# A four-layer block on one core: the layer norm of the next batch is taken later in the MLP stage

## The chip, the cores and the metric

One core of a Trainium2 chip runs one program. The time is that of the device in microseconds (us), the median of three runs. TensorE is called PE (its weight loads PEld), VectorE DVE, ScalarE ACT, GpSimd POOL, SyncE SP. The program is one long chain of stages, parted by barriers, so that what a stage takes longer the program takes longer.

## The reference

Four layers follow each other on x of 8 batches x 256 tokens x 512 features: an attention to a context, an attention over channels, a transformer layer (self attention, cross attention, MLP), and a recurrent block. The change is in the MLP of the third:

```python
ln_out = layernorm(x, ln3_s, ln3_b)
mlp_out = gelu(ln_out @ w1 + b1) @ w2 + b2      # w1: 512 x 2048, w2: 2048 x 512
return x + mlp_out
```

## The kernel before

`token_mlp` is the stage. It goes over the 8 batches (256 rows each) one after the other, and in each over 8 chunks of 256 hidden features. Every engine has its own instruction queue, written out by hand in the order of `for b, n in order(...)`: b is the batch, n the chunk. Products are made in three passes of rounded high and low parts (`_hi`, `_lo`), and so each operand has to be split on DVE or POOL ahead of the product.

In chunk n PE makes `hidden(b, n)` (24 matmuls, L2212), then, in two chunks of each batch, a `turn` (4 transposes, L2199) of the normalised rows of the next batch, then `outputs` of the chunk three back (12 matmuls, L2227), as `Y_LAG` is 3; so outputs(b, 4) is the last of batch b ahead of hidden(b+1, 0), and outputs(b, 5) to (b, 7) stand in the first chunks of b+1. `hidden(b, 0)` first waits for `ln_split` of its batch.

For a chunk of hidden, ACT evicts the sums (`evict`, L2267 and L2270) as the values `pre` and their squares; DVE makes 0.044715 times the square plus 1 (called squared1 here, L2374); POOL multiplies by `pre` (cube, L2183); ACT takes the tanh (`bend`, L2276); DVE multiplies (`gelu`, L2366); ACT rounds (`round_hidden`, L2281); POOL takes the rest (`split_hidden`, L2158). In chunk n each engine does squared1, cube and evict of n, and bend, gelu, rounding and rest of n-1.

The layer norm of the next batch b+1 is made beside batch b: SP loads its rows (L2122); DVE takes `statistics` (L2315) and `moment` (L2322), POOL the power -0.5 (`power`, L2166), DVE `normalise` (L2329) into xn; PE turns xn in two halves; ACT keeps each half with the scale and bias applied (`keep_turned`, L2253); DVE splits it (`split_turned`: a cast at L2336, a subtraction at L2338, which raises `ln_split`). `TURN_STEPS` names the two chunks in which the turns stand; the splits stand one chunk behind them. `add_bias` on POOL (L2170) adds the last bias to the rows, and in batch 0 it waits for all weights to be split, since it writes where they were staged; the load of batch b+2 waits for it.

Batch 0 has more to do. Of the weights the first two quarters of w1 are there when the stage begins. The rest comes in twelve halves of 512 KB through three staging buffers, in this order:

```python
HALVES = [(n, i, k) for n, i in (("w2", 0), ("w1", 2), ("w2", 1), ("w1", 3), ("w2", 2), ("w2", 3)) for k in range(2)]
```

SP loads them (L2132; the load of batch 1's rows stands behind half 4), ACT rounds two of them in each of chunks 0 to 5 (L2259), and DVE splits two in the same chunk (L2348), behind its gelu and ahead of its layer norm work. The load of half k, from 3 on, waits for the split of half k-3. PE waits for the halves that it needs: hidden 4 for halves 2 and 3, hidden 6 for 6 and 7, outputs 0, 2, 4 and 6 for 0 and 1, 4 and 5, 8 and 9, 10 and 11.

Of the kernel before, what the change touches and what calls it, by code (L numbers as in the profile page):

```python
# [12 lines left out]
BATCH, TOK, FEAT = 8, 256, 512  # L13
# [33 lines left out]
def make_identity(pool, ident, sem):  # L47

    pool.memset(ident[:, :], 0.0).then_inc(sem, 1)
    pool.wait_ge(sem, 1)  # L50
    pool.affine_select(out=ident[:, :], in_=ident[:, :], compare_op=ALU.not_equal, fill=1.0, base=0,
                       pattern=[[-1, P]], channel_multiplier=1).then_inc(sem, 1)
# [1975 lines left out]
def token_mlp(nc, semaphores, x, w1_d, w2_d, ln_cols, b1, b2, out, ahead, here, following):  # L2028
# [4 lines left out]
    Y_LAG = 3  # L2033

    HALVES = [(n, i, k) for n, i in (("w2", 0), ("w1", 2), ("w2", 1), ("w1", 3), ("w2", 2), ("w2", 3)) for k in range(2)]
    TURN_STEPS = (2, 4)
    with ExitStack() as ctx:
        def sb(name, shape, dtype=F32):
            return ctx.enter_context(nc.sbuf_tensor("mlp_" + name, shape, dtype))
# [46 lines left out]
        def of(b, per_batch, k, unit=1):  # L2086

            return at(b + 2, per_batch, k, unit)

        def piece_of(i, part):  # L2090
            return (w1_hi, w1_lo)[part][:, :, i * FEAT:(i + 1) * FEAT]
# [7 lines left out]
        def order(drain):  # L2099

            for g in range(BATCH * CHUNKS + drain):
                yield g // CHUNKS, g % CHUNKS

        def before(b, n, steps):
            g = b * CHUNKS + n - steps
            return g // CHUNKS, g % CHUNKS
# [42 lines left out]
        @block.gpsimd  # L2149
        def _(pool):  # L2150
            make_identity(pool, ident, ident_made)
            pool.memset(half_power[:, :], -0.5).then_inc(const_made, 1)
            pool.memset(eps[:, :], 1e-5).then_inc(const_made, 1)
            pool.wait_ge(const_made, 2)

            def split_hidden(b, k):
                pool.wait_ge(hid_rounded, of(b, CHUNKS, k))
                pool.tensor_tensor(hid_lo[k % RING][:, :, :], pre[k % RING], hid_hi[k % RING][:, :, :].bitcast(F32),  # L2158
                                   ALU.subtract).then_inc(hid_split, 1)

            def power(b):
                pool.wait_ge(counted, of(b, 2, 1))
                pool.wait_ge(normalised, of(b - 1, 1, 0))
                pool.tensor_tensor(var_eps[:, :], moments[:, :, 1], eps[:, :], ALU.add).then_inc(powered, 1)
                pool.wait_ge(powered, of(b, 2, 0))
                pool.tensor_tensor(rstd[:, :], var_eps[:, :], half_power[:, :], ALU.pow).then_inc(powered, 1)  # L2166

            def add_bias(b):
                pool.wait_ge(added, of(b - 1, 1, 0))
                pool.tensor_tensor(xb, xs[b % 2][:, :, :], b2_row[:, :].unsqueeze(1).to_broadcast([P, TT, FEAT]),  # L2170
                                   ALU.add).then_inc(biased, 1)

            power(0)
            pool.wait_ge(cols_loaded, 48)
            for b, n in order(1):
                if b == 0 and n == 6:
                    pool.wait_ge(half_split, len(HALVES))
                    add_bias(b)
                elif 0 < b < BATCH and n == Y_LAG + 1:
                    add_bias(b)  # L2180
                if b < BATCH:
                    pool.wait_ge(squared1, of(b, CHUNKS, n))
                    pool.tensor_tensor(cube[n % RING], cube[n % RING], pre[n % RING], ALU.mult).then_inc(cubed, 1)  # L2183
                if b or n:
                    split_hidden(*before(b, n, 1))
                if n == 0 and b + 1 < BATCH:
                    power(b + 1)

        @block.tensor
        def _(pe):  # L2190
# [45 lines left out]
            for b, n in order(Y_LAG):  # L2236
                if b < BATCH:
                    if n == 0:
                        pe.wait_ge(ln_split, of(b, 2, 1))
                    hidden(b, n)  # L2240
                if n in TURN_STEPS and b + 1 < BATCH:
                    turn(b + 1, TURN_STEPS.index(n))
                if b or n >= Y_LAG:
# [3 lines left out]
        def _(act):  # L2247
# [45 lines left out]
            for b, n in order(1):  # L2293
# [7 lines left out]
                if b or n:  # L2301
                    round_hidden(*before(b, n, 1))
                if n in TURN_STEPS and b + 1 < BATCH:
                    keep_turned(b + 1, TURN_STEPS.index(n))
                if 0 < b < BATCH and n == Y_LAG:
# [4 lines left out]
        @block.vector  # L2310
        def _(dve):
            def statistics(b):
                dve.wait_ge(loaded[b % 2], 16 * (b // 2 + 1))
                for m in range(TT):
                    ins = dve.bn_stats(stats[:, m, :], xs[b % 2][:, m, :])  # L2315
                ins.then_inc(counted, 1)

            def moment(b):
                dve.wait_ge(counted, of(b, 2, 0))
                dve.wait_ge(normalised, of(b - 1, 1, 0))  # L2320
                for m in range(TT):
                    ins = dve.bn_aggr(moments[:, m, :], stats[:, m, :])  # L2322
                ins.then_inc(counted, 1)

            def normalise(b):
                dve.wait_ge(powered, of(b, 2, 1))
                dve.wait_ge(turned, of(b - 1, 2, 1))
                for m in range(TT):
                    ins = dve.tensor_scalar(xn[:, m, :], xs[b % 2][:, m, :], moments[:, m, 0:1], rstd[:, m:m + 1],  # L2329
                                            ALU.subtract, ALU.mult)  # L2330
                ins.then_inc(normalised, 1)

            def split_turned(b, i):
                here = slice(2 * i, 2 * i + 2)
                dve.wait_ge(turned_kept, of(b, 2, i))
                dve.tensor_copy(ln_hi[b % 2][:, here, :], ln_raw[:, here, :]).then_inc(ln_rounded, 1)  # L2336
                dve.wait_ge(ln_rounded, of(b, 2, i))
                dve.tensor_tensor(ln_lo[b % 2][:, here, :], ln_raw[:, here, :], ln_hi[b % 2][:, here, :].bitcast(F32),  # L2338
                                  ALU.subtract).then_inc(ln_split, 1)

            def split_piece(i):
                dve.wait_ge(piece_hi, i + 1)
                dve.tensor_tensor(piece_of(i, 1), ahead.pieces[i][:, :, :], piece_of(i, 0).bitcast(F32),
                                  ALU.subtract).then_inc(piece_split, 1)

            def split_half(k):
                dve.wait_ge(half_hi, k + 1)
                dve.tensor_tensor(half_of(k, 1), stages[k % 3], half_of(k, 0).bitcast(F32), ALU.subtract).then_inc(half_split, 1)  # L2348

            statistics(0)  # L2350
            moment(0)
            normalise(0)
            split_piece(0)
            split_turned(0, 0)
            split_turned(0, 1)
            split_piece(1)
            def add_rows(b):
                dve.wait_ge(y_used, of(b, CHUNKS, CHUNKS - 1))
                dve.wait_ge(biased, of(b, 1, 0))
                dve.wait_ge(stored, of(b - 1, 1, 0, 16))  # L2360
                dve.scalar_tensor_tensor(out=res, in0=ps_y[:, :, :], scalar=0.5, in1=xb,
                                         op0=ALU.mult, op1=ALU.add).then_inc(added, 1)

            def gelu(b, k):
                dve.wait_ge(bent, of(b, CHUNKS, k))
                dve.scalar_tensor_tensor(out=pre[k % RING], in0=cube[k % RING], scalar=1.0,  # L2366
                                         in1=pre[k % RING], op0=ALU.add, op1=ALU.mult).then_inc(gelled, 1)

            for b, n in order(1):
                if 0 < b < BATCH and n == Y_LAG:  # L2370
                    add_rows(b - 1)
                if b < BATCH:
                    dve.wait_ge(squared, of(b, CHUNKS, n))
                    dve.tensor_scalar(cube[n % RING], cube[n % RING], 0.044715, 1.0, ALU.mult, ALU.add).then_inc(squared1, 1)  # L2374
                if b or n:
                    gelu(*before(b, n, 1))
                if b == 0 and n < len(HALVES) // 2:
                    split_half(2 * n)
                    split_half(2 * n + 1)
                if b + 1 < BATCH:  # L2380
                    if n == 0:
                        statistics(b + 1)
                        moment(b + 1)
                    elif n == 1:
                        normalise(b + 1)
                    elif n - 1 in TURN_STEPS:
                        split_turned(b + 1, TURN_STEPS.index(n - 1))
            add_rows(BATCH - 1)
# [1104 lines left out]
```

## Time and profile before

| | |
|---|---|
| median of three runs | 3719.94 us (3717.66 to 3721.94) |
| the profiled execution | 3721.94 us, its span 3719.9 us |
| PE busy | 3444.8 us (93% of the span) |
| DVE busy | 2339.9 us (63%) |
| POOL busy | 2012.5 us (54%) |
| ACT busy | 1835.1 us (49%) |
| mean granted clock of PE | 0.969 |
| the MLP stage | PE's first matmul at 2348.46 us, the last store issued at 2744.77 us |

Times in the rows are microseconds from the start of the span. Matmuls overlap, so the time from one start to the next says how long one takes, and the printed duration is longer. The granted clock is a share of 2.4 GHz; there are two levels, 0.5 and 1. In a row of a timeline the bracket tells how long the engine sat idle ahead of the instruction, and for what. DVE's printed durations overlap the next start by some 0.08 us.

### The profile page before, as it was taken

The page shows a single profiled execution, that of the slowest core. Times are in us where ns is not written, and L with a number is a line of the kernel's source. Part 1 is how long each engine was busy: PE and PEld are TensorE (multiplying, and loading weights), DVE is VectorE, ACT ScalarE, POOL GpSimd, SP SyncE. Part 2 cuts the span into 40 slices and gives each one's busy share as a digit, 9 for nine tenths or more (in the row PEclk, how much of TensorE's full clock was granted, in tenths as well). Part 3 has the DMA queues.
Part 4 walks back from the last instruction along what each step waited for, and adds up shares of the span by engine and source line. Part 5 has one row for each costly group of instructions (what it writes and reads, how often), then busy time and mean ns, then how long its engine had stood idle before and what let it go on. Part 6 is the DMA issues. An engine that isn't in the chain of part 4 may idle for free. (4 is left out here: it accounts for less than half of the span.)

```text
span 3719.9 us, 59815 instructions
## 1 busy us (share of the span) xinstructions
PE 3444.8 (93%) x23544; PEld 2669.8 (72%) x23544; DVE 2339.9 (63%) x2892; ACT 1835.1 (49%) x4242; POOL 2012.5 (54%) x1088
## 2 busy tenths in 40 slices
PE   8989999999999999979989998799987888889978
PEld 6878778877877887558877776699975655656544
DVE  2455665565566556657778787555535677787776
ACT  2134664565456446556766776455532333333322
POOL 2235665575567556425556666355534566666653
PEclk9999999999999999989999999799998899999989
DMA  4231211121122111120021111200040000000000
GB/s 139 98 128 46 81 57 59 58 70 58 48 70 69 59 46 58 39 98 33 30 75 52 41 41 55 88 23 24 18 147 6 13 18 1 18 18 18 13 18 12
DMA packets 114302, 189.91 MB, mean 51 GB/s; under 512 B 17904, under 2 KB 36848, under 8 KB 113392
## 3 DMA queue, kind: packets, MB, share of 16 engines
q1 hardware_dynamic: 111856, 182.00, 14.4%
q8 instruction: 183, 3.00, 0.3%
q10 hardware_dynamic: 2176, 4.19, 0.3%
q14 instruction: 87, 0.71, 0.1%
HBM read 161.01 MB, written 25.17 MB: 50 GB/s over the span
## 5 line engine op out<-in xcount | busy, mean ns | idle before, releaser
L1025 POOL TENSOR_TENSOR l_pr<-l_pr,l_inv 128x1024 f32<-128x1024 f32 x256 | 479.8, 1895 | 383.6 <-DVE l_inv L1087 383.6
L895 ACT ACTIVATE l_pr<-l_ps_s,l_top 128x512 f32<-128x512 f32 x512 | 348.6, 690 | 353.0 <-DVE l_top L1083 271.9
L1529 POOL TENSOR_TENSOR tok_pr<-tok_pr,tok_ma 128x1024 f32<-128x1024 f32 x128 | 304.4, 2400 | 280.2 <-DVE tok_pr L1907 280.2
L2790 POOL TENSOR_TENSOR rec_rs<-rec_sE,rec_rT 128x1024 f32<-128x1024 f32 x128 | 326.7, 2555 | 215.8 <-DVE rec_sE L3278 166.8
L1020 POOL TENSOR_TENSOR l_x_lo<-ahead_piece,l_x_hi 128x1024 fp32r<-128x1024 f32 (+1 forms) x97 | 294.0, 3031 | 154.2 <-ACT l_x_hi L879 154.2
L1083 DVE TENSOR_REDUCE l_top<-l_ps_s 128x2 f32<-128x1024 f32 x256 | 304.1, 1218 | 10.5 <-PE l_ps_s L669 10.5
L3278 DVE TENSOR_TENSOR_SCAN rec_sE<-rec_wE,rec_ps_v 128x1024 f32<-128x1024 f32 x128 | 292.7, 2287 | 5.5 <-POOL rec_rs L2790 1.1
L679 PE MATMUL l_ps_t<-l_ident,l_pr 128*128 128x128 f32 x2048 | 275.3, 277 | 10.8 <-POOL l_pr L1025 4.8
L679 PEld LDWEIGHTS l_ps_t<-l_ident,l_pr 128*128 128x128 f32 x2048 | 225.6, 141 | 78.1 <-issue 60.7
L1779 ACT ACTIVATE tok_pr<-tok_pr,tok_shift 128x256 f32<-128x256 f32 x512 | 253.7, 498 | 15.8 <-DVE tok_shift L1915 14.5
L630 PE MATMUL l_ps_b<-l_x_hi,l_w_lo 128*128 128x256 f32 x784 | 226.7, 289 | 0.0
L630 PE MATMUL l_ps_b<-l_x_hi,l_w_hi 128*128 128x256 f32 x784 | 221.2, 282 | 0.0
L630 PE MATMUL l_ps_b<-l_x_lo,l_w_hi 128*128 128x256 f32 x784 | 221.0, 282 | 0.0
L3275 DVE TENSOR_TENSOR rec_ps_v<-rec_ps_v,rec_kT 128x1024 f32<-128x1024 f32 x128 | 156.7, 1225 | 72.5 <-ACT rec_kT L3143 71.5
L1915 DVE TENSOR_REDUCE tok_shift<-tok_pr 128x4 f32<-128x1024 f32 x128 | 155.5, 1216 | 47.6 <-POOL tok_pr L1529 45.5
L1091 DVE COPY l_pT<-l_ps_t 128x512 f32<-128x512 f32 x256 | 174.3, 681 | 2.9 <-PE l_ps_t L679 2.6
L900 ACT ACTIVATE l_pT<-l_ps_t 128x512 f32<-128x512 f32 x256 | 152.5, 596 | 22.7 <-PE l_ps_t L679 22.6
L1615 PE MATMUL tok_ps_t<-tok_ident,tok_pr 128*128 128x128 f32 x1024 | 138.7, 279 | 24.7 <-DVE tok_pT L1920 17.5
L1907 DVE TENSOR_TENSOR tok_pr<-tok_ps_s,tok_mk 128x1024 f32<-128x1024 f32 x128 | 155.7, 1217 | 5.3 <-PE tok_ps_s L1604 5.3
L1615 PEld LDWEIGHTS tok_ps_t<-tok_ident,tok_pr 128*128 128x128 f32 x1024 | 113.6, 142 | 54.9 <-issue 35.8
L657 PE MATMUL l_ps_b<-l_wv_lo,l_x_hi 128*128 128x256 f32 x512 | 149.4, 292 | 3.5 <-DVE l_wv_lo L1074 2.1
L630 PEld LDWEIGHTS l_ps_b<-l_x_hi,l_w_lo 128*128 128x128 f32 x784 | 148.2, 189 | 2.7 <-issue 1.0
(507 smaller groups left out, 9752.3 us busy)
## 6 DMA issues: line engine op xcount, KB each, us to landing
ahead_piece<-x SPq DMA_DIRECT2D x63, 512.0 KB, 3.9
ahead_piece<-in_c SPq DMA_DIRECT2D x63, 512.0 KB, 4.7
ahead_rows<-x SPq DMA_DIRECT2D x22, 512.0 KB, 3.8
ahead_piece<-in_L_w_qk SPq DMA_DIRECT2D x16, 512.0 KB, 6.0
x<-tok_xb SPq DMA_DIRECT2D x16, 512.0 KB, 2.8
l_xt<-in_xT SPq DMA_DIRECT2D x8, 512.0 KB, 6.5
l_ct<-in_cT SPq DMA_DIRECT2D x8, 512.0 KB, 7.6
l_xn<-in_x SPq DMA_DIRECT2D x8, 512.0 KB, 4.8
```

The lines of the kernel that those rows point to most:

```text
L630: mm = pe.matmul(bank[:, here], w[:, part, half * SLOTS + s, :], x[b % 2][:, s, here], start=(s == 0 and w is w_lo), stop=(s == SLOTS - 1 ...
L679: mm = pe.transpose(ps_t[h][:, m, :], pr[t][:, h, m * P:(m + 1) * P], ident[:, :])
L895: act.activation(pr[t][:, h, :], ps_s[:, t % 2, h, :], ACT.Exp, bias=top[:, t, h:h + 1], accum_out=mass[:, t, h:h + 1]).then_inc(exped, 1)
L1020: pool.tensor_tensor(x_lo[b % 2][:, which, :], rows, x_hi[b % 2][:, which, :].bitcast(F32), ALU.subtract).then_inc(x_split, 2 if source is ...
L1025: pool.tensor_tensor(pr[t][:, :, :], pr[t][:, :, :], inv[:, t, :].unsqueeze(2).to_broadcast([P, 2, FEAT]), ALU.mult).then_inc(scaled, 1)
L1083: dve.tensor_reduce(top[:, t, :], ps_s[:, t % 2, :, :], AXIS.X, ALU.max, negate=True).then_inc(topped, 1)
L1091: dve.tensor_copy(pT[1][:, :, t * P:(t + 1) * P], ps_t[1][:, :, :]).then_inc(turned_kept[1], 1)
L1529: pool.tensor_tensor(tile, tile, ma[u][:, :, :].rearrange("p t k -> p (t k)").unsqueeze(1).to_broadcast([P, 2, TT * TOK]), ALU.add).then_i ...
L1615: mm = pe.transpose(ps_t[:, i, t, m * P:(m + 1) * P], pr[n % RING][:, i, m, t * P:(t + 1) * P], ident[:, :])
L1779: ins = act.activation(tile, tile, ACT.Exp, bias=shift[n % RING][:, i, m:m + 1], accum_out=mass[n // 2 % 2][:, m, n % 2 * 2 + i:n % 2 * 2 ...
L2790: pool.tensor_tensor(rs[j % 2][:, :, :], sE[j % 2][:, :, :], rT[s][:, :, :], ALU.mult).then_inc(rs_made, 1)
L3278: dve.tensor_tensor_scan(sE[j % 2][:, :, :].rearrange("p c t -> p (c t)"), wE[s][:, :, :].rearrange("p c t -> p (c t)"), ps_v[j % 2][:, :, ...
```

## The change

The layer norm work of the next batch is put later within a batch: statistics and moment, and the power on POOL, from chunk 0 to chunk 1; normalise from chunk 1 to 2; the two turns (with keep_turned) from chunks 2 and 4 to 4 and 6; and so the two split_turned from chunks 3 and 5 to 5 and 7. In batch 0, add_bias on POOL goes from chunk 6 to chunk 7. No instruction is added or taken away.

```diff
@@ -2033,7 +2033,7 @@
     Y_LAG = 3
 
     HALVES = [(n, i, k) for n, i in (("w2", 0), ("w1", 2), ("w2", 1), ("w1", 3), ("w2", 2), ("w2", 3)) for k in range(2)]
-    TURN_STEPS = (2, 4)
+    TURN_STEPS = (4, 6)
     with ExitStack() as ctx:
         def sb(name, shape, dtype=F32):
             return ctx.enter_context(nc.sbuf_tensor("mlp_" + name, shape, dtype))
@@ -2173,7 +2173,7 @@
             power(0)
             pool.wait_ge(cols_loaded, 48)
             for b, n in order(1):
-                if b == 0 and n == 6:
+                if b == 0 and n == 7:
                     pool.wait_ge(half_split, len(HALVES))
                     add_bias(b)
                 elif 0 < b < BATCH and n == Y_LAG + 1:
@@ -2183,7 +2183,7 @@
                     pool.tensor_tensor(cube[n % RING], cube[n % RING], pre[n % RING], ALU.mult).then_inc(cubed, 1)
                 if b or n:
                     split_hidden(*before(b, n, 1))
-                if n == 0 and b + 1 < BATCH:
+                if n == 1 and b + 1 < BATCH:
                     power(b + 1)
 
         @block.tensor
@@ -2378,10 +2378,10 @@
                     split_half(2 * n)
                     split_half(2 * n + 1)
                 if b + 1 < BATCH:
-                    if n == 0:
+                    if n == 1:
                         statistics(b + 1)
                         moment(b + 1)
-                    elif n == 1:
+                    elif n == 2:
                         normalise(b + 1)
                     elif n - 1 in TURN_STEPS:
                         split_turned(b + 1, TURN_STEPS.index(n - 1))
```

## Rows read from the trace of the kernel before

**Rows 1.** Busy time by stretch: us, PE, PEld, DVE, ACT, POOL, clock, DMA share, GB/s

```profile
2366.00:2388.00 22.00, 6.70 (x37) 6.52 (x37) 14.20 (x16) 9.18 (x16) 9.09 (x6) 0.61 0.46 140
...
2520.00:2560.00 40.00, 40.00 (x260) 36.15 (x259) 20.33 (x23) 20.78 (x46) 20.90 (x16) 1.00 0.07 27
```

**Rows 2.** Waits in the stage: total us, times, longest

```profile
ACT ahead_piece L2267 <- PE mlp_ps_h L2212: 58.2, 60, 3.6
...
PE mlp_ps_t L2199 <- DVE mlp_xn L2329: 15.3, 1, 15.3
```

**Rows 3.** Timeline of PE, batch 0: start, us, instruction, idle before

```profile
2366.76 0.28 PE L2212 MATMUL mlp_ps_h<-mlp_ln_hi,mlp_w_hi 128*128 128x256 f32 x1
2382.34 1.08 PE L2199 MATMUL mlp_ps_t<-mlp_ident,mlp_xn 128*128 128x128 f32 x4 [15.30 <-DVE mlp_xn L2329]
2383.07 0.56 PE L2212 MATMUL mlp_ps_h<-mlp_ln_hi,mlp_w_lo 128*128 128x256 f32 x1
...
2413.82 0.28 PE L2212 MATMUL mlp_ps_h<-mlp_ln_hi,mlp_w_lo 128*128 128x256 f32 x1
```

**Rows 4.** Timeline of DVE, batch 0

```profile
2374.51 1.29 DVE L2315 BATCH_NORM_STATS2 mlp_stats<-mlp_xs 128x6 f32<-128x512 f32 x2 [7.34 <-DMA mlp_xs<-x]
...
2380.26 1.94 DVE L2329 TENSOR_SCALAR mlp_xn<-mlp_xs,mlp_moments,mlp_rstd 128x512 f32<-128x512 f32 x2
2382.12 0.41 DVE L2374 TENSOR_SCALAR ahead_piece<-ahead_piece 128x512 f32<-128x512 f32 x1
...
2383.06 2.29 DVE L2348 TENSOR_TENSOR mlp_w_lo<-mlp_xb_res,mlp_w_hi 128x1024 fp32r<-128x1024 f32 x1
2385.27 2.30 DVE L2348 TENSOR_TENSOR mlp_w_lo<-mlp_spare,mlp_w_hi 128x1024 fp32r<-128x1024 f32 x1
2389.88 0.43 DVE L2374 TENSOR_SCALAR ahead_piece<-ahead_piece 128x512 f32<-128x512 f32 x1 [2.31 <-ACT ahead_piece L2270]
...
2407.86 2.79 DVE L2338 TENSOR_TENSOR mlp_ln_lo<-mlp_ln_raw,mlp_ln_hi 128x512 fp32r<-128x512 f32 x1
```

**Rows 5.** Timeline of the queue of SP, batch 0

```profile
2367.62 0.46 SPq L2122 DMA_DIRECT2D mlp_xs<-x  x1
```

**Rows 6.** Timeline of PE, steady batch: hidden, outputs, hidden begin

```profile
2488.73 0.28 PE L2212 MATMUL mlp_ps_h<-mlp_ln_hi,mlp_w_lo 128*128 128x256 f32 x1
...
2491.55 0.40 PE L2227 MATMUL mlp_ps_y<-mlp_w_lo,mlp_hid_hi 128*128 128x512 f32 x1
...
2494.36 0.28 PE L2212 MATMUL mlp_ps_h<-mlp_ln_hi,mlp_w_lo 128*128 128x256 f32 x1
```

**Rows 7.** Timeline of ACT and DVE in the same steady batch

```profile
2491.76 0.84 ACT L2267 ACTIVATE ahead_piece<-mlp_ps_h,mlp_b 128x256 f32<-128x256 f32 x2 [0.72 <-PE mlp_ps_h L2212]
...
2493.36 0.43 DVE L2374 TENSOR_SCALAR ahead_piece<-ahead_piece 128x512 f32<-128x512 f32 x1 [3.89 <-ACT ahead_piece L2270]
2493.88 1.82 DVE L2366 SCALAR_TENSOR_TENSOR ahead_piece<-ahead_piece 128x512 f32<-128x512 f32 x1
2495.63 0.41 DVE L2336 CAST mlp_ln_hi<-mlp_ln_raw 128x512 fp32r<-128x512 f32 x1
2496.07 0.69 DVE L2338 TENSOR_TENSOR mlp_ln_lo<-mlp_ln_raw,mlp_ln_hi 128x512 fp32r<-128x512 f32 x1
```

**Rows 8.** Timeline of POOL, batch 0: add_bias

```profile
2407.49 2.61 POOL L2170 TENSOR_TENSOR mlp_xb_res<-ahead_rows,mlp_b 128x1024 f32<-128x1024 f32 x1
```

**Rows 9.** Timelines of DVE and PE where PE waited for a split

```profile
2357.55 0.69 DVE L2338 TENSOR_TENSOR mlp_ln_lo<-mlp_ln_raw,mlp_ln_hi 128x512 fp32r<-128x512 f32 x1
...
2358.29 0.39 PE L2212 MATMUL mlp_ps_h<-mlp_ln_hi,mlp_w_lo 128*128 128x256 f32 x1
```

**Rows 10.** Context stage: a wait of PE, and stretches as in rows 1

```profile
78.87 0.50 PE L163 MATMUL l_ps_d<-l_cv_hi,l_prT_lo 128*128 128x512 f32 x1 [2.56 <-DVE l_prT_lo L375]
...
78.90:83.90 5.00, 5.00 (x18) 4.14 (x19) 2.53 (x3) 0.00 (x0) 5.00 (x3) 0.66 0.62 190
118.70:123.70 5.00, 5.00 (x31) 4.49 (x32) 3.23 (x3) 0.00 (x0) 5.00 (x3) 1.00 0.58 188
```

## Prediction

> **What bounds the kernel now.** I read the page first for the shares (PE 93% of the span), then the busy time by stretch for the one stage that the diff touches, then who waited for whom in it, and last the timeline of single instructions. In the body of the stage PE is busy in 40.00 of 40.00 us at the full clock, DVE in 20.33 and POOL in 20.90 [rows 1]. So a microsecond of stall on PE is a microsecond of the program, and work on DVE or POOL is free as long as nothing on PE waits for it. Of the waits, ACT's for PE's sums (58.2 us in 60 waits) is the mark of a stage that PE paces; the only long wait of PE itself is one of 15.3 us for xn [rows 2].
>
> That wait belongs to batch 0. PE has run chunks 0 to 2 of hidden by 2366.8, reaches turn(1, 0), and starts it only at 2382.34. The next chunk of hidden begins at 2383.07, and hidden(1, 0), the first work of batch 1, at 2413.82 [rows 3]. DVE shows why: statistics(1) waits 7.34 us for the rows of batch 1, which SP issued at 2367.62 behind two halves of weights [rows 4, 5], starts at 2374.51, and normalise(1) follows at 2380.26, behind the next chunk and two splits of weights [rows 4].
>
> **What the change does at the start.** Everything is one chunk later for statistics and normalise, and two later for the turns. The rows of batch 1 still land when they did, since SP's order is the same: DVE is held at statistics(1) until about 2374.5 again. But in front of that wait it has now done chunk 1's squared1 and gelu and the splits of halves 2 and 3, which before came after it. Behind it come chunk 2, halves 4 and 5, and normalise(1): the same list with each number one higher. So normalise(1) ends, and turn(1, 0) starts, near 2382.3 as before. The difference is what PE has done by then: hidden 3, outputs 0 and hidden 4 lie ahead of the turn, 3 x 2.81 us (outputs takes 2494.36 - 2491.55 = 2.81 us, hidden 2491.55 - 2488.73 = 2.82, [rows 6]). Before, the first of these, hidden 3, even ran for the most part at the lower clock of 1.2 GHz (the mean granted over 2366 to 2388 is 0.61 of 2.4 GHz, [rows 1]), behind PE's long wait.
>
> Does PE keep this? From 2382.34 it has left: two turns (about 0.4 each), four outputs and three hiddens, 7 x 2.81 + 0.8 = 20.5 us, so it could be at hidden(1, 0) at 2402.8. But it waits there for ln_split, that is for split_turned(1, 1) on DVE. DVE's list between 2382.1 and that split was, before, four chunks, eight halves and both split_turned, ending 2407.86 + 2.79 = 2410.65 [rows 4]. Now it is five chunks, six halves and the same two splits. Two halves less is 2 x 2.21 = 4.4 us (2383.06 to 2385.27), DVE's wait of 2.31 at 2389.88 (for the sums that PE made at half clock) is gone, and a chunk more is 0.94 (2382.12 to 2383.06, when its inputs are ready, [rows 4]) to 2.27 (2493.36 to 2495.63, when POOL's cube runs beside it, [rows 7]): 2404.9 to 2406.2. And chunk 7's squared1 now stands between the turn and the split: behind gelu 5 ACT rounds, keeps the turned half and evicts, and DVE waits for all three. Before, that wait was 3.89 us behind chunk 4, of which ACT itself waited 0.72 for PE; 3.2 us remain, since PE is ahead now [rows 7]. That gives 2408.1 to 2409.4; I take 2408.8, and so **5.0 us** gained at hidden(1, 0) against 2413.82. The bounds: 8.5 at best (2402.8 plus the 2.5 us of the next part), nothing at worst.
>
> add_bias(0) moves on POOL from chunk 6 to chunk 7. Before, it ran at 2407.49 for 2.61 us, and the split beside it took 2.79 instead of 0.69 us [rows 4, 7, 8]. It will again run just ahead of that split, so I leave its 2.1 us in. The Trainium skill (SBUF — State Buffer, Who interferes with whom) has GpSimd and certain VectorE instructions take one port pair in turn for a whole instruction; the trace agrees, as the split ends only after add_bias does. By that rule a collision costs up to the full 2.61 us, and the gain would be 5.0 with it and some 7.1 without.
>
> **What the change does at every batch's end.** This is the part I hold to be decisive. hidden(b+1, 0) comes after outputs(b, 4), and waits for both halves of ln. Before, the second split_turned was done at chunk 5, with two chunks in hand. Now it stands in chunk 7, the last, behind that chunk's squared1 and gelu. The trace has exactly this pattern one step early: at chunk 5 of a batch, a step behind a turn. PE ends its hidden at 2491.55, does outputs, and wants the next hidden at 2494.36 [rows 6]. ACT evicts at 2491.76, squared1 runs at 2493.36, gelu at 2493.88 (1.82 us), the cast at 2495.63 and the second half of the split at 2496.07 [rows 7]. From the start of that instruction to PE's start is 0.74 us, where PE did wait for it (2357.55 to 2358.29, [rows 9]): 2496.81. So PE stalls 2496.81 - 2494.36 = **2.45 us**. Nothing else is in PE's queue that it could do: outputs(b, 5) stands behind hidden(b+1, 0). Behind the stalled hidden wait ACT's next evict, and through it DVE and POOL, so all shift together and the pattern repeats. There are seven boundaries; the first is in the sum above, six remain: 6 x 2.45 = 14.7 us. Bounds of one: 1.1 if squared1 and gelu take 0.94 instead of 2.27 (above), and 4.5 if the split takes 2.79 as beside add_bias [rows 4].
>
> **The clock.** PE's stall in this dense work can lower its clock. The context stage has four waits of 2.56 us in dense matmuls; behind the one that ended at 78.87 the granted clock over 5 us was 0.66, so two thirds of the 5 us ran at 1.2 instead of 2.4 GHz, while behind the one at 118.7 it was 1.00 [rows 10]. One such fall is 0.34 x 5 = 1.7 us of full-speed work lost. I take two falls in six, 3.4 us; bounds 0 and 6 x 1.7 = 10.2.
>
> **What costs nothing.** In batches 1 to 6 statistics and moment (1.29 us and a trifle) move into chunk 1 and normalise (at most 1.94, [rows 4]) into chunk 2; DVE is idle half of the time there, PE needs xn only at chunk 4, and POOL's power moves with them. Without that cover each would still have two chunks, 11 us, before the turn. The turn instructions on PE are the same number. The load of batch 2 waits for add_bias(0), which now comes at about 2407 and not 2407.49, and its first reader stands a chunk later. No DMA is added.
>
> **Sum.** -5.0 + 14.7 + 3.4 = +13.1 us. The profiled execution took 3721.94; 3735.0 by it. The median of the three runs is 3719.94, 2.0 lower, so 3733.
>
> **Rivals.**
> - The clock falls at nearly every boundary: -5.0 + 14.7 + 10.2 = +19.9, 3740. For it: the fall behind 78.87. Against: the 1.00 behind an equal wait. 0.14.
> - Batch 0 gives nothing back, since weights or DVE hold it as long as before: 14.7 + 3.4 = +18.1, 3738. For it: halves are chained through DVE, ACT and loads. Against: PE is two sets further by 2382, and two halves are already split. This is also the case in which the change does not remove the wait but moves it. 0.10.
> - Batch 0 gives all of 8.5 and no fall of the clock: +6.2, 3726. 0.10.
> - The other side: the stall at the boundary does not come, because the last split is done before PE wants it. Then only batch 0 counts, -5.0 to -11.0 (8.5 and the first boundary's 2.45), 3709 to 3715. It decides only if the chain from evict to split, 5.0 us, fits in outputs' 2.8; even with the shorter pair it takes 3.7. With the whole 8.5 gained, a stall under 0.2 us would be needed to be faster by 0.2%. 0.07.
> - My forecast, around +13: 0.59.
>
> **Numbers.** 0.2% of this kernel is 7.4 us, about what can be told from no change: slower means over 3727.4, faster under 3712.5. From the cases: slower 0.75 (forecast, clock, nothing back, less some where batch 0 gives more), same 0.17, faster 0.08. The range runs from 3722 (batch 0's best, smaller stalls) to 3742 (clock at most boundaries); the last case and the extremes, about 2 in 10, are left out.
>
> **What would show it.** In the profile after: the 15.3 us wait of PE for xn shrinks to one of about 3 us at turn(1, 0), near the same time 2382; PE waits about 2.5 us, seven times, in front of L2212 for L2338 on DVE, once per batch at a pitch of 48.3 us (8 x 5.63 for the sets, 0.8 for two turns, and the stall); hidden(1, 0) starts near 2409; the clock over some of the 5 us behind the stalls is under 1.00. The prediction is wrong if those waits are missing or under 1 us, if hidden(1, 0) starts well before 2405, or if DVE's rows of batch 1 land later than 2374.5 because half 5 is now issued beside them.

## The result, and the profile after

The changed kernel takes 3744.06 us (median of four runs, 3743.09 to 3751.37), against 3720.94 before on the same chip: 1.0066 times as long, interval 1.0048 to 1.0084, so slower by 0.66% and clear of the noise. The forecast had the direction; the time lies 2 us over its range of 3722 to 3742. The profiled execution took 3744.32 us, 22.4 more than that of before.

The page of the changed kernel, its span and the busy time of the engines:

```profile
span 3742.3 us, 59815 instructions
...
PE 3457.7 (92%) x23544; PEld 2678.3 (72%) x23544; DVE 2332.8 (62%) x2892; ACT 1833.5 (49%) x4242; POOL 2011.9 (54%) x1088
```

PE is busy 13 us longer with the same 23544 matmuls: more of them ran at the lower clock. The waits within the stage (total us, times, longest):

```profile
PE mlp_ps_h L2212 <- DVE mlp_ln_lo L2338: 20.6, 8, 6.8
...
PE mlp_ps_y L2227 <- POOL mlp_hid_lo L2158: 4.7, 2, 4.2
...
PE mlp_ps_y L2227 <- DVE mlp_xb_res L2361: 2.7, 6, 0.5
...
DVE mlp_stats L2315 <- DMA mlp_xs<-x: 2.0, 1, 2.0
...
PE mlp_ps_t L2199 <- DVE mlp_xn L2329: 0.4, 1, 0.4
```

The wait of 15.3 us for xn is 0.4 now [rows 2], and DVE waits 2.0 and not 7.3 us for the rows of batch 1 [rows 4]. In their place stand eight waits of PE for the last split (one of them is the wait of batch 0's start, 0.2 us), and six for L2361, add_rows, which nobody had forecast.

To leave out what differs between two runs ahead of the stage (the profile after reaches it 2.7 us sooner), I take the stage by itself: from PE's first matmul in it to the first of the next stage. Before, on PE's timeline:

```profile
2348.46 0.90 PE L59 MATMUL mlp_ps_h<-mlp_ident 128*128 128x128 f32 x3 [5.39 <-POOL mlp_ident L51]
...
2749.27 1.11 PE L59 MATMUL rec_ps_acc<-rec_ident 128*128 128x128 f32 x4 [5.79 <-POOL rec_ident L51]
```

After, with the starts of outputs 0, the first turn and hidden(1, 0):

```profile
2345.78 1.54 PE L59 MATMUL mlp_ps_h<-mlp_ident 128*128 128x128 f32 x6 [5.39 <-POOL mlp_ident L51]
...
2370.90 0.77 PE L2227 MATMUL mlp_ps_y<-mlp_w_lo,mlp_hid_hi 128*128 128x512 f32 x1 [4.25 <-POOL mlp_hid_lo L2158]
...
2379.46 0.63 PE L2199 MATMUL mlp_ps_t<-mlp_ident,mlp_xn 128*128 128x128 f32 x4 [0.38 <-DVE mlp_xn L2329]
...
2406.97 0.58 PE L2212 MATMUL mlp_ps_h<-mlp_ln_hi,mlp_w_lo 128*128 128x256 f32 x1 [6.75 <-DVE mlp_ln_lo L2338]
...
2771.17 1.12 PE L59 MATMUL rec_ps_acc<-rec_ident 128*128 128x128 f32 x4 [5.78 <-POOL rec_ident L51]
```

So the stage took 2749.27 - 2348.46 = 400.81 us and takes 2771.17 - 2345.78 = 425.39: 24.6 more. hidden(1, 0) starts 61.19 us behind the first matmul, and started at 2413.82 - 2348.46 = 65.36 [rows 3]: batch 0 gives 4.2 back, where 5.0 was forecast. DVE's timeline in batch 0 shows what hidden(1, 0) waits for:

```profile
2371.59 1.28 DVE L2315 BATCH_NORM_STATS2 mlp_stats<-mlp_xs 128x6 f32<-128x512 f32 x2 [1.96 <-DMA mlp_xs<-x]
...
2377.35 1.97 DVE L2329 TENSOR_SCALAR mlp_xn<-mlp_xs,mlp_moments,mlp_rstd 128x512 f32<-128x512 f32 x2
...
2397.59 0.69 DVE L2366 SCALAR_TENSOR_TENSOR ahead_piece<-ahead_piece 128x512 f32<-128x512 f32 x1
2401.34 1.90 DVE L2374 TENSOR_SCALAR ahead_piece<-ahead_piece 128x512 f32<-128x512 f32 x1 [3.07 <-ACT ahead_piece L2270]
2403.16 0.68 DVE L2366 SCALAR_TENSOR_TENSOR ahead_piece<-ahead_piece 128x512 f32<-128x512 f32 x1
2403.77 1.48 DVE L2336 CAST mlp_ln_hi<-mlp_ln_raw 128x512 fp32r<-128x512 f32 x1
2405.28 1.63 DVE L2338 TENSOR_TENSOR mlp_ln_lo<-mlp_ln_raw,mlp_ln_hi 128x512 fp32r<-128x512 f32 x1
```

Its rows come at 2371.59, normalise at 2377.35 and the turn at 2379.46, as the forecast had it (33.7 us into the stage, 33.9 before). At the end DVE waits 3.07 us between gelu 5 and squared1 of chunk 7, and from there squared1 (1.90 us, 0.42 in the chunk before), the cast (1.48) and the subtraction (1.63) are long, each beside an instruction of POOL. PE stands idle for 6.75 us.

A later boundary, as batch 4 ends and batch 5 begins, on PE: outputs(4, 4), hidden(5, 0), the next outputs, outputs(5, 0) and hidden(5, 4):

```profile
2604.39 0.40 PE L2227 MATMUL mlp_ps_y<-mlp_w_lo,mlp_hid_hi 128*128 128x512 f32 x1
...
2609.63 0.38 PE L2212 MATMUL mlp_ps_h<-mlp_ln_hi,mlp_w_lo 128*128 128x256 f32 x1 [2.28 <-DVE mlp_ln_lo L2338]
...
2612.57 0.40 PE L2227 MATMUL mlp_ps_y<-mlp_w_lo,mlp_hid_hi 128*128 128x512 f32 x1
...
2630.07 0.50 PE L2227 MATMUL mlp_ps_y<-mlp_w_lo,mlp_hid_hi 128*128 128x512 f32 x1 [0.45 <-DVE mlp_xb_res L2361]
...
2632.97 0.28 PE L2212 MATMUL mlp_ps_h<-mlp_ln_hi,mlp_w_lo 128*128 128x256 f32 x1
```

and on DVE: chunk 7 with the split, then chunk 2 with normalise and add_rows:

```profile
2606.19 0.43 DVE L2374 TENSOR_SCALAR ahead_piece<-ahead_piece 128x512 f32<-128x512 f32 x1 [3.73 <-ACT ahead_piece L2270]
2606.71 1.81 DVE L2366 SCALAR_TENSOR_TENSOR ahead_piece<-ahead_piece 128x512 f32<-128x512 f32 x1
2608.44 0.41 DVE L2336 CAST mlp_ln_hi<-mlp_ln_raw 128x512 fp32r<-128x512 f32 x1
2608.89 0.69 DVE L2338 TENSOR_TENSOR mlp_ln_lo<-mlp_ln_raw,mlp_ln_hi 128x512 fp32r<-128x512 f32 x1
...
2625.62 0.43 DVE L2374 TENSOR_SCALAR ahead_piece<-ahead_piece 128x512 f32<-128x512 f32 x1 [1.81 <-ACT ahead_piece L2270]
...
2627.89 0.99 DVE L2329 TENSOR_SCALAR mlp_xn<-ahead_rows,mlp_moments,mlp_rstd 128x512 f32<-128x512 f32 x2
2628.80 1.21 DVE L2361 SCALAR_TENSOR_TENSOR mlp_xb_res<-mlp_ps_y,mlp_xb_res 128x1024 f32<-128x1024 f32 x1
```

In the kernel before, at the same place of a batch, add_rows on DVE and outputs of chunk 3 on PE:

```profile
2523.77 1.21 DVE L2361 SCALAR_TENSOR_TENSOR mlp_xb_res<-mlp_ps_y,mlp_xb_res 128x1024 f32<-128x1024 f32 x1
...
2525.76 0.40 PE L2227 MATMUL mlp_ps_y<-mlp_w_lo,mlp_hid_hi 128*128 128x512 f32 x1
```

The reader is to see two things. From outputs to hidden PE takes 2609.63 - 2604.39 = 5.24 us, and took 2.81 [rows 6]: 2.43 of stall for the split that starts at 2608.89. And in chunk 3 outputs waits until add_rows, 1.21 us from 2628.80, has emptied the sums; add_rows stands behind normalise in DVE's queue; before, it ended 0.8 us ahead of outputs. The clock, by stretches of 5 us behind two of the stalls (columns as in rows 1):

```profile
2457.50:2462.50 5.00, 4.94 (x27) 4.85 (x28) 0.00 (x1) 0.28 (x1) 1.14 (x1) 0.66 0.00 0
...
2609.60:2614.60 5.00, 4.97 (x33) 4.60 (x34) 0.23 (x1) 1.83 (x5) 1.11 (x1) 1.00 0.00 0
```

Behind five of the six short stalls, and behind the long one, the granted clock is 0.66 to 0.68; behind the one at 2609.6 it is 1.00. hidden(5, 0) there takes 2612.57 - 2609.63 = 2.94 us; behind the others the same 24 matmuls take 4.16 to 4.46. Where they take 4.16, the outputs behind them are slow too: from one hidden(b, 0) to the next (called the pitch of a batch) it is 49.17 us behind 2609.63 and 50.67 to 50.70 behind the other four that a batch follows, so one fall of the clock costs 1.5 us.

### The profile page after: what moved, and what is told of

Its sections match the earlier page's. It is cut to its first block and busy times, and to the rows that moved or that the text cites. A ratio compares the mean times of both kernels' runs of the same rounds, so it can differ in the third digit from the quotient of the medians.

```text
span 3742.3 us, 59815 instructions
## 1 busy us (share of the span) xinstructions
PE 3457.7 (92%) x23544; PEld 2678.3 (72%) x23544; DVE 2332.8 (62%) x2892; ACT 1833.5 (49%) x4242; POOL 2011.9 (54%) x1088
## 3 DMA queue, kind: packets, MB, share of 16 engines
q10 hardware_dynamic: 2176, 4.19, 0.3%
## 5 line engine op out<-in xcount | busy, mean ns | idle before, releaser
L1083 DVE TENSOR_REDUCE l_top<-l_ps_s 128x2 f32<-128x1024 f32 x256 | 303.9, 1217 | 10.6 <-PE l_ps_s L669 10.5
L679 PE MATMUL l_ps_t<-l_ident,l_pr 128*128 128x128 f32 x2048 | 275.5, 277 | 10.7 <-POOL l_pr L1025 4.6
L1779 ACT ACTIVATE tok_pr<-tok_pr,tok_shift 128x256 f32<-128x256 f32 x512 | 253.7, 497 | 15.7 <-DVE tok_shift L1915 14.6
L2212 PE MATMUL mlp_ps_h<-mlp_ln_hi,mlp_w_lo 128*128 128x256 f32 x512 | 148.1, 289 | 20.6 <-DVE mlp_ln_lo L2338 20.6
L2183 POOL TENSOR_TENSOR ahead_piece<-ahead_piece 128x512 f32<-128x512 f32 x64 | 87.5, 1368 | 140.3 <-DVE ahead_piece L2374 140.3
L2374 DVE TENSOR_SCALAR ahead_piece<-ahead_piece 128x512 f32<-128x512 f32 x64 | 31.1, 486 | 198.4 <-ACT ahead_piece L2270 198.4
```

The source lines that it names most:

```text
L679: mm = pe.transpose(ps_t[h][:, m, :], pr[t][:, h, m * P:(m + 1) * P], ident[:, :])
L1083: dve.tensor_reduce(top[:, t, :], ps_s[:, t % 2, :, :], AXIS.X, ALU.max, negate=True).then_inc(topped, 1)
L1779: ins = act.activation(tile, tile, ACT.Exp, bias=shift[n % RING][:, i, m:m + 1], accum_out=mass[n // 2 % 2][:, m, n % 2 * 2 + i:n % 2 * 2 ...
```

## The experiments

The times are medians on the chip, beside runs of the kernel before on the same chip (3720.2 to 3721.2 in these), to which the ratios belong. Stages are from PE's first matmul of the stage to that of the next, each in one profile; "hidden(1, 0)" is its start from that first matmul. Four profiles with the same order in batch 0 (changed, first_batch_only, statistics_back, filled_stall) have it at 61.2 to 61.6. Many of the intervals of the ratios overlap, so small differences between two of the kernels are read from the rows of the stage and not from the whole time.

| kernel | time, us | ratio to before, interval | stage | hidden(1, 0) |
|---|---|---|---|---|
| before | 3719.94 | 1 | 400.8 | 65.4 |
| changed | 3744.06 | 1.0066 [1.0048, 1.0084] | 425.4 | 61.2 |
| first_batch_only | 3717.71 | 0.9991 [0.9982, 1.0] | 398.2 | 61.3 |
| later_batches_only | 3745.52 | 1.0076 [1.0062, 1.009] | 424.5 | - |
| statistics_back | 3740.29 | 1.0057 [1.0044, 1.0071] | 418.2 | 61.6 |
| turns_4_5 | 3715.72 | 0.9992 [0.9983, 1.0001] | 395.2 | 55.3 |
| filled_stall | 3740.51 | 1.0052 [1.0038, 1.0066] | 417.9 | 61.2 |
| split_ahead | 3719.97 | 0.9998 [0.9989, 1.0007] | 400.0 | 58.6 |
| first_batch_4_5 | 3711.20 | 0.9977 [0.9968, 0.9987] | 391.5 | 56.0 |
| rows_before_half_3 | 3712.29 | 0.998 [0.9971, 0.9989] | 393.2 | 57.8 |
| bias_at_6 | 3743.45 | 1.0061 [1.0049, 1.0073] | 426.9 | 62.5 |
| rows_early_turns_3_5 | 3709.14 | 0.997 [0.9959, 0.9981] | 389.8 | 54.4 |
| rows_early_turns_4_5 | 3711.91 | 0.9973 [0.9964, 0.9983] | 390.3 | 54.8 |

**first_batch_only** takes the change in batch 0 alone (statistics and power stand in the chunk STATISTICS(b), normalise in NORMALISE(b)):

```diff
-    TURN_STEPS = (4, 6)
+    TURN_STEPS = lambda b: (4, 6) if b == 0 else (2, 4)
+    STATISTICS = lambda b: 1 if b == 0 else 0
+    NORMALISE = lambda b: 2 if b == 0 else 1
```

> The change in batch 0 alone; batches 1 to 7 keep the order of before. Theory (three costs at each later boundary, a gain in batch 0): hidden(1, 0) starts 61.2 us behind PE's first matmul of the stage instead of 65.4, one fall of the clock of 1.5 us behind the long stall in front of it, nothing after: 2.7 us under before, 3718. Rival (batch 0 gives nothing back once the noise of its loads is taken out, and the gain of 4.2 us was read from one profile): within 1 us of before.

```profile
2347.27 1.12 PE L59 MATMUL mlp_ps_h<-mlp_ident 128*128 128x128 f32 x4 [5.39 <-POOL mlp_ident L51]
...
2408.55 0.58 PE L2214 MATMUL mlp_ps_h<-mlp_ln_hi,mlp_w_lo 128*128 128x256 f32 x1 [6.51 <-DVE mlp_ln_lo L2340]
...
2745.51 0.90 PE L59 MATMUL rec_ps_acc<-rec_ident 128*128 128x128 f32 x3 [5.79 <-POOL rec_ident L51]
```

398.2 us, 2.6 less than before; hidden(1, 0) starts at 61.3, and no wait follows it. In the stage the gain of batch 0 is there and small: 4.1 us sooner at hidden(1, 0), less 1.5 for the fall of the clock behind the long stall. By the whole time, 0.9991, the interval just reaches 1.0, so it is barely told from none.

**later_batches_only** is its complement (turns in 2 and 4 for b = 0, in 4 and 6 for the rest, and so on, add_bias(0) in chunk 6).

> Batch 0 as before, batches 1 to 6 changed. Theory: six stalls of PE of 2.43 us in front of hidden(b+1, 0) with 0.12 us of restart (15.3), six of 0.74 us in chunk 3 for add_rows (4.4), and a fall of the clock of 1.5 us behind five of the six (7.6): 27.3 us over before, 3748. Rival (the falls and the chunk 3 stalls hang on a phase that batch 0 of the changed kernel set): 15.3 us over before, 3736.

PE's waits from 2400 to 2725:

```profile
PE mlp_ps_h L2214 <- DVE mlp_ln_lo L2340: 13.7, 6, 2.3
PE mlp_ps_y L2229 <- DVE mlp_xb_res L2363: 2.7, 6, 0.5
```

Six stalls of 2.3 and six of 0.5 us are there with batch 0 as it was, so they don't hang on it. The stage came 23.7 us over before, not 27.3: the clock fell behind three of the six stalls, not five, and one fall is 1.5 us (a pitch of 50.7 against 49.2). The times of both parts, -2.6 and +23.7, make 21.1 of the 24.6; two falls less account for most of the rest.

**statistics_back** puts statistics and power in chunk 0 and normalise in chunk 1 again for b > 0, with the turns still in 4 and 6:

```diff
+    STATISTICS = lambda b: 1 if b == 0 else 0
+    NORMALISE = lambda b: 2 if b == 0 else 1
```

> The changed kernel, but in batches 1 to 6 statistics, power and normalise are back in chunks 0 and 1; the turns stay in 4 and 6. Theory: normalise ahead of add_rows makes the stall of 0.74 us in chunk 3, so the six go and the other costs stay: 4.4 us under the changed kernel, 3739.7, and no wait of PE for L2361. Rival (that stall comes from the phase behind the boundary stall, or from the missing turn in chunk 2, which gave add_rows 0.4 us more): the waits stay or shrink only in part, 3742 to 3744.

```profile
PE mlp_ps_h L2214 <- DVE mlp_ln_lo L2340: 20.1, 7, 6.4
```

That is all of PE's waits there: the six for add_rows are gone, and the pitch of a batch without a fall is 48.44 us (2653.26 to 2701.70) against 49.17 (2609.63 to 2658.80): 0.73 us each. Statistics and power went back together with normalise, but statistics in chunk 1 can't be what delays add_rows: behind it DVE waits 1.81 us for ACT at squared1 of chunk 2 (2625.62 above). So normalise's place makes that stall. The stage is 7.2 us shorter, of which 4.4 is this, and the rest in the main that the clock fell behind three of the six short stalls and not five.

**turns_4_5** has `TURN_STEPS = (4, 5)` in the changed kernel and nothing else.

> The changed kernel with the second turn in chunk 5 instead of 6, so that the last split_turned stands in chunk 6. Theory: all stalls in front of hidden(b+1, 0) go (6.75 + 6 x 2.55), and with them the falls of the clock (7 x 1.5); the six of 0.74 us stay: 3744.1 - 6.8 - 15.3 - 10.5 = 3711.5, 9 us faster than before. Rival (the falls of the clock come from the 0.46 us waits or from elsewhere, not from these stalls): 3722, and the clock still falls in most batches.

PE's two kinds of waits, at hidden(1, 0) and at outputs(1, 0):

```profile
2395.98 0.39 PE L2212 MATMUL mlp_ps_h<-mlp_ln_hi,mlp_w_lo 128*128 128x256 f32 x1 [1.34 <-DVE mlp_ln_lo L2338]
...
2416.41 0.50 PE L2227 MATMUL mlp_ps_y<-mlp_w_lo,mlp_hid_hi 128*128 128x512 f32 x1 [0.45 <-DVE mlp_xb_res L2361]
```

No wait stands at the six later boundaries, the clock is 1.00 from 2410 to 2730, and the stage is 395.2, 30.2 us less than changed (32.6 expected: hidden(1, 0) comes 5.9 sooner and not 6.8, as 1.3 us of wait stayed, and there were six falls to save, not seven). Six waits for add_rows stay, without any boundary stall ahead of them. The second turn's place, one chunk, carries more than the whole loss of 24.6; what is left of the change gains 5.6 us of stage on the kernel before. The whole time (0.9992, its interval reaches 1.0001) doesn't show that gain clearly, and the 9 us that were expected didn't come.

**split_ahead** leaves the turns in 4 and 6, but in chunk 7 DVE does the split first:

```diff
             for b, n in order(1):
+                if n == 7 and b + 1 < BATCH:
+                    split_turned(b + 1, 1)
...
-                    elif n - 1 in TURN_STEPS:
-                        split_turned(b + 1, TURN_STEPS.index(n - 1))
+                    elif n == 5:
+                        split_turned(b + 1, 0)
```

> The changed kernel with one instruction pair moved: in chunk 7 DVE does split_turned(b+1, 1) ahead of squared1 and gelu and not behind them; the turns stay in chunks 4 and 6. Theory (the stall is the place of the split behind squared1 and gelu, not the place of the turn): no stall at the six boundaries, about 1.5 us left at the first, no falls of the clock; the six of 0.74 us stay. Stage about 395 us as with the turns in chunks 4 and 5, 3715. Rival (a turn in chunk 6 is too late for ACT and PE as well): a stall of 1 us or more at each boundary, stage over 402.

DVE in a later batch (split, then squared1 of chunk 7), and the last split of batch 0:

```profile
2450.01 0.71 DVE L2336 CAST mlp_ln_hi<-mlp_ln_raw 128x512 fp32r<-128x512 f32 x1 [1.61 <-ACT mlp_ln_raw L2253]
2450.76 0.69 DVE L2338 TENSOR_TENSOR mlp_ln_lo<-mlp_ln_raw,mlp_ln_hi 128x512 fp32r<-128x512 f32 x1
2452.12 0.43 DVE L2376 TENSOR_SCALAR ahead_piece<-ahead_piece 128x512 f32<-128x512 f32 x1 [0.67 <-ACT ahead_piece L2270]
...
2402.10 2.72 DVE L2338 TENSOR_TENSOR mlp_ln_lo<-mlp_ln_raw,mlp_ln_hi 128x512 fp32r<-128x512 f32 x1
```

The split is done at 2451.4, squared1 starts at 2452.12 unhindered, and PE waits at no later boundary. A turn in chunk 6 is early enough; it was the queue that made the split late. At the first boundary the guess of 1.5 us was wrong: 3.3 stayed, since the split took 2.72 us beside add_bias, and the clock fell behind that stall (0.66 over 5 us). The stage is 400.0 and not 395, much as before the change.

**filled_stall** lets PE work in the stall:

```diff
                     if n == 0:
+                        if b:
+                            pe.wait_ge(turned_kept, of(b, 2, 1))
+                            keep_busy(pe, ps_t[0][:, 0, 0:P], ident, 18)
                         pe.wait_ge(ln_split, of(b, 2, 1))
```

> The changed kernel, and PE makes 18 transposes of the identity into a bank that nobody reads, in front of its wait for ln_split in batches 1 to 7, so that it works in most of the stall. Theory (the clock falls because PE is idle there): hidden(b+1, 0) starts at the same times as far as DVE sets them, the 1.5 us falls behind the six short stalls go, and the stage from PE's first matmul to that of the next stage takes some 9 us less than the 425.4 of the changed kernel: 3735. Rival (the falls have another cause, such as the waits of 0.46 us in chunk 3, which stay): no less than 423, 3742 to 3744.

The second hidden(b, 0) behind the transposes, and the stretch from 2410 to 2730, then the same stretch of the changed kernel:

```profile
2460.36 0.39 PE L2212 MATMUL mlp_ps_h<-mlp_ln_hi,mlp_w_lo 128*128 128x256 f32 x1 [0.33 <-DVE mlp_ln_lo L2341]
...
2410.00:2730.00 320.00, 315.31 (x2038) 283.86 (x2039) 145.29 (x171) 151.81 (x335) 156.40 (x121) 1.00 0.05 19
```

```profile
2410.00:2730.00 320.00, 303.57 (x1890) 272.29 (x1890) 142.70 (x169) 149.66 (x330) 153.89 (x119) 0.97 0.05 19
```

The mean clock of the stretch goes from 0.97 to 1.00, all later batches have a pitch of 49.18 us, and the stage is 7.5 us shorter, though each boundary still takes as long and PE has more to do. That is five falls of 1.5 us; the 9 us expected counted six. At hidden(1, 0) the 18 transposes left 4.19 us of wait, and behind it the clock still fell (0.67 over 5 us). The whole times alone (1.0052 and 1.0066, with intervals that overlap) wouldn't tell the two kernels apart. The cause of the falls behind the short stalls is PE's idleness in them. The Trainium skill (TensorE: Matmul & The Clock Gate, What's actually happening) says that the clock gate is set by how busy PE has been recently; the trace agrees, with a mean of 0.97 where PE idled at the six boundaries and 1.00 where they were filled. Over four kernels with these stalls (changed, later_batches_only, statistics_back, bias_at_6) the clock fell behind 16 of 24 short ones, 3 to 5 of six in each, and behind none of six once they were filled. Which of them it spares stays open.

**first_batch_4_5** joins the late turns of batch 0, in 4 and 5, with the old order from batch 1 on.

> Batch 0 with statistics in chunk 1, normalise in 2 and turns in 4 and 5; batches 1 to 6 as in the kernel before. Theory (all that the late turns are worth lies in batch 0, and all later costs in the later batches): hidden(1, 0) 55.3 us behind PE's first matmul of the stage, then a pitch of 45.9 and no waits: stage 400.8 - 10.0 = 390.8 us, 10 us faster than before, 3710. Rival (the later batches need the late places too once batch 0 is shorter, for the rows of batch 2 land late): the gain is under 6 us.

The stage is 391.5, hidden(1, 0) comes at 56.0, and PE waits 0.86 us there and nowhere in batches 1 to 7 behind it. It is faster than both kernels (0.9977 of before).

**rows_before_half_3** is the kernel before with one line of SP moved:

```diff
+            load(1)
             for k in range(3, len(HALVES)):
                 load_half(k)
-                if k == 4:
-                    load(1)
```

> The kernel before with one DMA moved in SP's order: the rows of batch 1 are loaded behind the first three halves, ahead of halves 3 and 4. Theory (the wait of 15.3 us hangs in its first half on the rows' landing at 2374.5, 7.3 us of DVE idle): the wait of PE for xn shrinks by about 7 us, and hidden(1, 0) comes 4 to 9 us earlier: 3712 to 3716. Rival (halves 3 and 4 are the bound, and the rows are hidden behind them): the wait shrinks, hidden(1, 0) by under 2 us, no faster than 3719.

```profile
2366.75 0.66 PE L2198 MATMUL mlp_ps_t<-mlp_ident,mlp_xn 128*128 128x128 f32 x2 [7.91 <-DVE mlp_xn L2328]
```

DVE no longer waits for the rows at all, and half of the 15.3 us is gone; the other 7.91 is DVE's own queue up to the end of normalise, with the splits of halves 0 to 3 in it and a wait of 1.01 us for half 3. The one moved load gains nearly as much as the best rearrangement of batch 0 (7.6 us of stage against 9.3).

**bias_at_6** puts add_bias(0) back in chunk 6 of the changed kernel.

> The changed kernel with add_bias(0) back in chunk 6 on POOL. In the changed kernel add_bias(0) ran at 2400.63 for 2.33 us, and squared1 of chunk 7 beside it took 1.90 instead of 0.43 us, in front of the split that PE waits for. Theory (the place of add_bias costs 1.5 us of the first boundary's stall): the wait of 6.75 us at hidden(1, 0) becomes 5.3, or more if add_bias now holds up chunk 6's cube; the stage 424 to 425 us. Rival (it only moves what it delays): 425.4, no change.

DVE's second instruction of the first split, and hidden(1, 0):

```profile
2395.92 2.78 DVE L2338 TENSOR_TENSOR mlp_ln_lo<-mlp_ln_raw,mlp_ln_hi 128x512 fp32r<-128x512 f32 x1
...
2406.14 0.58 PE L2212 MATMUL mlp_ps_h<-mlp_ln_hi,mlp_w_lo 128*128 128x256 f32 x1 [5.85 <-DVE mlp_ln_lo L2338]
```

The first split now takes 2.78 us beside add_bias in place of the last, and the wait of PE is 5.85. hidden(1, 0) comes 1.35 us later than in the changed kernel, but not by add_bias: the first split begins at 51.9 us of the stage, against 50.4, before add_bias has run. From there to the end of the second split DVE takes 10.6 us (2395.47 to 2406.09) and took 10.7 (2396.20 to 2406.91). So the rival holds, the place of add_bias changes nothing, and the shorter wait of PE only means that PE too was later. The collision can be moved, not shed.

**rows_early_turns_3_5** and **rows_early_turns_4_5** join the early load with late turns of batch 0 (statistics and normalise in chunks 0 and 1 for the first, 1 and 2 for the second; from batch 1 on as before).

> Rows of batch 1 loaded ahead of half 3, statistics and normalise in chunks 0 and 1 everywhere as before, the turns of batch 0 in chunks 3 and 5, those of later batches in 2 and 4. Theory (with the rows there, one chunk of delay for the turns is enough, and PE makes hidden 3 and outputs 0 in the 7.9 us that it waited in the kernel with the early rows alone): hidden(1, 0) 52 to 54 us behind PE's first matmul of the stage, against 65.4 before, 57.8 with early rows alone and 56.0 with late turns alone; stage 388 us, 3708. Rival (DVE's and ACT's list of weights is the bound by then): 56 us or more, no better than either alone.

> Rows of batch 1 loaded ahead of half 3; batch 0 with statistics in chunk 1, normalise in 2, turns in 4 and 5; later batches as before. Theory: statistics finds its rows at once, so the early rows give little beside the late turns: hidden(1, 0) 53 to 55.5 us behind PE's first matmul, stage 389 to 391, 3709. Rival: the halves land earlier too, and it beats the turns in 3 and 5.

The turn of the first of them:

```profile
2376.47 0.89 PE L2200 MATMUL mlp_ps_t<-mlp_ident,mlp_xn 128*128 128x128 f32 x4 [5.06 <-DVE mlp_xn L2330]
```

In the stage both gain 1 to 4 us over the load alone and over the turns in 4 and 5 alone (the turns in 3 and 5 alone were not run); by the whole time they can't be told from first_batch_4_5 (0.9977). The first has the lowest time here, 0.997 (0.9959 to 0.9981), 11 us under before; but hidden(1, 0) at 54.4 us is at the late end of what was expected, and PE still waits 5.06 us for xn. The load alone is worth 7.6 us of stage and the turns in 4 and 5 alone 9.3, and both together 10.5: they take the same idle time.

## Why the prediction came out as it did

By its own steps:

- **Batch 0, -5.0 us**: measured -4.2, hidden(1, 0) at 61.2 instead of 65.4. The argument that DVE's list repeats with numbers one higher held: turn(1, 0) came at the same place, and DVE's wait of 3.07 us ahead of chunk 7 was put at 3.2. Of the wait of DVE that it called gone (2.31 us) 1.51 stayed, at 2390.57, and squared1, cast and subtraction beside POOL took 3.5 us more than alone where 2.1 were set; other parts of the list were shorter, so that the sum came out within 0.8 us is partly luck. That PE would wait about 3 us at the turn was wrong; it waits 0.38, because outputs 0 had to wait 4.25 us for its first operand before, and ran at the lower clock behind that.
- **The stall at a boundary, 2.45 us**: measured 2.43 at each of the six, 14.6 us in all. Reading the chain one chunk early in the old trace gave it to two hundredths. A restart of 0.12 us (hidden 2.94 and not 2.82) was left out: 0.8 in all.
- **The clock, 3.4 us**: the term that was mis-sized. Five falls behind the six short stalls and one behind the long one, 9.0 us together (1.5 each by the pitch, 1.4 behind the long one). The price of one, 1.7, was a little high; the number, two in six, was far too low, and the long stall of batch 0 was left out of the count, although 6.0 us of idle PE followed from the forecast's own numbers (2402.8 to 2408.8; 6.75 came). filled_stall and turns_4_5 show that the falls come from the stalls.
- **"What costs nothing"**: the step that failed. It asked of normalise only whether xn would be ready for the turn, and not what stands behind normalise in DVE's queue. In chunk 2 it stands right in front of add_rows, for which outputs(b, 0) waits in chunk 3. Before, add_rows ended about 0.8 us ahead of that. normalise puts it 0.9 us later, and the turn gone from chunk 2 lets PE come 0.4 sooner: 0.73 us at each of six, 4.4, which the forecast put at nothing. statistics_back, in which only the turn is gone, has 0.35 of the 0.8 left (add_rows ends at 2672.72, outputs starts at 2673.07) and no stall; normalise in chunk 2 with the turn still there was not tried.

In sum -4.2 + 14.6 + 0.8 + 9.0 + 4.4 = 24.6 us, which is what the stage lost; the forecast was 13.1, and 10.0 of the 11.5 between them are the clock (5.6) and add_rows (4.4). The rival with a fall at nearly every boundary (+19.9) was right on the clock and lacks the 4.4. The rival in which no stall comes was wrong, and so was the one in which batch 0 gives nothing.

## What to carry to other kernels

In a hand-written order, a moved instruction has two neighbours to check: what waits for it, and what stands behind it in the new place. The slack of the first reader, here two chunks, was spent where nothing was to be had for it: the whole gain of the late places lay in batch 0 and most of the loss in the six batches behind it (even in batch 0 the second turn in chunk 6 and not 5 costs 5.9 us at hidden(1, 0)), and a place per batch, or one load sooner, keeps the one without the other. And a stall of an otherwise busy PE is to be priced with the clock that it can cost, here 1.5 us on top of 2.4, two times in three.

## What the hardware showed unexpectedly

A stall of 2.28 us between stretches in which PE does nothing but matmuls was followed by the lower clock 16 times in 24, and within one program with such a stall in every batch the clock was spared 1 to 3 times in six. And DVE's short instructions beside one of POOL can take several times as long, ending 0.3 to 0.6 us after it: squared1 took 1.90 us instead of 0.43 beside add_bias (which ended at 2402.96, squared1 at 2403.24), and a subtraction of 0.69 took 2.72, 2.78 and 2.79 in three kernels.
